# Weight loads ahead in groups of eight and four, and a new order for the first loads of a three-layer-plus-experts kernel

## The chip, the cores and the metric

The kernel runs on 1 core of one Trainium2 chip. The metric is the device time of one execution in microseconds (us), median of several runs. The engines are PE (TensorE, matmul), DVE (VectorE), ACT (ScalarE), POOL (GpSimd) and SP (SyncE, which here only issues DMAs); SPq and ACTq are the issuing sequencers of SP and ACT. Each engine works through its own list of instructions in order and waits on semaphores.

## The reference, cut to what matters

The input is 16 sequences of 256 tokens with 256 features. Four blocks follow each other, each behind a residual sum and a layernorm.

```
x = _layernorm(x + _L0_attn_ref(x, ...))   # projection by W_in, state-space scan in chunks, W_out
x = _layernorm(x + _L0_ffn_ref(x, ...))    # quantised gate/up/down, 704 hidden
x = _layernorm(x + _L1_attn_ref(x, ...))   # w_qkv, running sums over the tokens, swiglu with 1024 hidden
x = _layernorm(x + _L1_ffn_ref(x, ...))    # 16 experts, top 4 of each token, 448 hidden
def _L1_ffn_ref(x, W_up, W_gate, W_down, gate_inp):
    ...
    topv, topi = jax.lax.top_k(logits, K)
    w = jax.nn.softmax(topv.astype(jnp.float32), axis=-1).astype(x.dtype)
    ...
    u = jnp.einsum('nc,ehc->neh', xf, W_up)
    g = jnp.einsum('nc,ehc->neh', xf, W_gate)
    h = jax.nn.silu(g) * u
    y = jnp.einsum('neh,ech,ne->nc', h, W_down, dense_w)
```

## The kernel before, in words

The program has three blocks with a barrier of all engines between them.

`layers_block` computes the first three layers and the choice of experts, one sequence of 256 tokens (two tiles of 128) at a time. Each engine follows a list of its own, `ORDER`, written by hand; `run_skewed` goes through the list once a round. The first letter of an entry sets which sequence it works on: A the round's own, N, G+ or B3+ a later or earlier one, C two rounds back. So in round i the SP list does N0 (load of xT of sequence i+1), A0 (rows of x of sequence i), A2 (store of xg of sequence i), WL.0 to WL.5 (six pieces of the weights of expert i), C7 and C9 (stores of x3 and of its two bf16 parts, of sequence i-2) and CE.

Names that matter at the start. `loads` are eleven constants and weights (const is 1024 KB, w_in 1312 KB, w_out 512 KB) on the signal `setup_loaded`, for which PE, ACT and DVE wait before their first instruction. `loads_b` are ten weights of the later layers (w_sw alone 2048 KB, 6102 KB in all) on `weights_loaded`; they are first needed when sequence 0 reaches its second layer. `padding` and 17 stores of it fill the table `meta_dram`, with `padding_stored` waited for by the first scatter of POOL (D8). `xg` goes to DRAM and comes back as `xgs` by seven indirect gathers on POOL (AX), on the two signals `xgs_in`.

The weights of the experts are split into a high and a low bf16 part in the same rounds: SP loads a piece into `w_stage` (two buffers), ACT casts the high part (WH.k, line 998), DVE subtracts for the low part (WL.k, line 1476), SP stores it (`store_piece`) and right behind the store issues the load of the piece after next. ACT's list in the first round reads ... WH.0, A2S, F3, A2L, WH.1, A3, WH.2, WH.3, A3L, G1+ ...; A3L copies cb_cross and raises `cb_copied`, for which PE waits before A4.0 (the level matmuls of line 715) of the same sequence and before G1 of the next.

`experts_block` runs 144 tiles of 128 rows. For each, ACT loads its row of the table (`meta_in`), POOL gathers `xin`, SP turns it by a DMA transpose into `xh`, PE multiplies by the expert's weights in `w_all` (line 1656), SP turns the hidden part into `hh`, PE multiplies again (line 1671), POOL adds the rows into `sums_dram`. Tile i of the first sixteen waits for the weights of expert i. `load_weights` loads one expert by two DMAs of 896 and 448 KB. Before, experts 0 to 7 are loaded at the end of the round before the last, 8 to 13 behind the last stores of x (CE of sequence 15) and 14 and 15 at the start of `experts_block`. `combine_block` sums and normalises the rows at the end.

Of the kernel before, what the change touches and what calls it, by code (L numbers as in the profile page):

```python
# [24 lines left out]
P = 128  # L25
T = 256
NT = T // P
D = 256
DC = D // P
# [8 lines left out]
SH = 1024  # L38
# [12 lines left out]
EARLY_A, EARLY_B = 8, 14  # L51
# [120 lines left out]
def spread(ap, axis, n):  # L172
# [112 lines left out]
def layers_block(nc, ins, nseq, cap, ntile, ident, waited, small, base, table, meta_dram, x3_dram, sums_dram, split_ug, split_dn, xg_dram,  # L285
                 w_all, weights_in, w_start):
    with ExitStack() as ctx:
# [62 lines left out]
        w_sw = sb("w_sw", [P, DC, 2 * SH])  # L350
        w_so = sb("w_so", [P, SJ, D])
        x1 = sb("x1", [P, NT, D])
        x1T = sb("x1T", [P, DC, T])
        sg = sb("sg", [P, 2, T])
        hT = sb("hT", [P, SJ, T])
        x2 = sb("x2", [P, NT, D])
# [6 lines left out]
        den = sb("den", [P, NT, D])  # L363
        yc = sb("yc", [P, NT, D])
        assert nc.sbuf_base >= w_start + EARLY_B * WB
# [42 lines left out]
        def mat(k):  # L408
            return const[:, k, :]

        loads = [(const[:, :, :], ins["matrices"]), (ident, ins["matrices"][:, IDENT, :]), (small[:, :], ins["small"]),
                 (w_in[:, :, :], ins["w_in"].rearrange("(c p) n -> p c n", p=P)),
                 (dt_bias[:, :], ins["dt_bias"]), (neg_a[:, :], ins["a_log"]),
                 (bc_bias[:, :, :], ins["bc_bias"]), (chosen_rows[:, :], ins["chosen_rows"]), (halves[:, :, :, :], ins["halves"]), (right[:, :], ins["right"]),
# [10 lines left out]
                   (w_route[:, :, :], ins["w_route"].rearrange("(c p) n -> p c n", p=P))]  # L425
        setup_loaded = sig("setup_loaded", 16 * len(loads))
# [105 lines left out]
        def _(sp):  # L532
            sp_carrier = Carrier(sp, waited)
            for to, src in loads:
                sp.dma_start(to, src).then_inc(setup_loaded.sem, 16)

            def load_x(s):

                if later(s):
                    sp.wait_ge(z_projected.sem, z_projected.before(s))  # L540
                sp.dma_start(xT[:, :, :], ins["xT"].rearrange("(c p) t -> p c t", p=P)[:, :, bass.ds(s * T, T)]
                             ).then_inc(xT_in.sem, 16)

            def load_rows(s):
# [5 lines left out]
                if isinstance(s, int) and s == 0:  # L550
                    for to, src in loads_b:
                        sp.dma_start(to, src).then_inc(weights_loaded.sem, 16)
                    load_piece(0, 0)
                    load_piece(0, 1)

                    sp.dma_start(padding[:, :, :], ins["empty"]).then_inc(padding_in.sem, 16)
                    sp.wait_ge(nothing_set.sem, nothing_set.at(0))
                    for sums in sums_dram:
                        sp.dma_start(sums[nseq * T:nseq * T + P, :], nothing[:, 0:D]).then_inc(sums_cleared.sem, 16)
                    sp.wait_ge(padding_in.sem, padding_in.at(0))  # L560
                    for e in range(NE + 1):
                        sp.dma_start(meta_dram[e * cap:(e + 1) * cap, :].rearrange("(p i) w -> p i w", p=P),
                                     padding[:, :, :]).then_inc(padding_stored.sem, 16)
# [38 lines left out]
            def store_xg(s):  # L602
# [1361 lines left out]
```

## Time and profile before

| | |
|---|---|
| median of 3 runs | 2052.14 us (2052.07 to 2055.04) |
| the profiled execution | 2062.8 us, its span 2061.0 us |
| PE busy | 1773.3 us, 86% |
| DVE busy | 1320.1 us, 64% |
| POOL busy | 859.4 us, 42% |
| ACT busy | 730.7 us, 35% |
| DMA queue of SP | 171.79 MB, 32.5% of the 16 engines |
| DMA queue of POOL | 67.40 MB, 17.8% |

The span is the time from the first to the last instruction that the profile holds. Busy shares are averages over the three blocks, which have different limits: the first block ends near 1431 us of the span, the experts fill the rest up to the short last block.

### The profile page before, as it was taken

To read this page: it belongs to the slowest core of one execution; us is meant where nothing else is said; L and a number is where in the kernel's file an instruction comes from. 1 tells how busy PE (TensorE), PEld (TensorE's weight loads), DVE (VectorE), ACT (ScalarE), POOL (GpSimd) and SP (SyncE) were. 2 spreads that over 40 slices of the span, in tenths; PEclk is the share of its full clock that TensorE was granted. 3 is DMA by queue.
4 is the path that set the end of the run, shared out by engine and by line. 5 is a ranking of instruction groups with operands and counts; after the bars stand their busy time and mean duration, and the time that the engine had idled before them with its cause. 6 is when DMAs were issued, how large, how long until landed. Compare 5 with 4: busy or idle time off the path is not lost. (4 is left out here: it accounts for less than half of the span.)

```text
span 2061.0 us, 34901 instructions
## 1 busy us (share of the span) xinstructions
PE 1773.3 (86%) x8724; PEld 1226.6 (60%) x8725; DVE 1320.1 (64%) x2876; ACT 730.7 (35%) x1384; POOL 859.4 (42%) x856
## 2 busy tenths in 40 slices
PE   3589999989999899899998998872799999999980
PEld 2257667667576576676765766652456566666650
DVE  3778878778787788787877887621334444444445
ACT  3234344344343443443444434220222223233223
POOL 2123243333432432334324323222466676666654
PEclk8799999999999999999999999986899999999995
DMA  8123132231231321312313313277799999999997
GB/s 288 56 92 108 28 116 71 65 107 58 80 106 32 109 83 51 107 58 86 107 37 97 99 35 103 67 182 221 143 161 172 173 172 175 174 175 178 172 152 250
DMA packets 385800, 244.37 MB, mean 119 GB/s; under 512 B 269072, under 2 KB 364624, under 8 KB 385360
## 3 DMA queue, kind: packets, MB, share of 16 engines
q1 hardware_dynamic: 319952, 171.79, 32.5%
q0 software_dynamic: 40704, 67.40, 17.8%
q10 hardware_dynamic: 25088, 4.50, 1.2%
q8 instruction: 26, 0.43, 0.1%
q14 instruction: 30, 0.25, 0.0%
HBM read 119.23 MB, written 67.73 MB: 91 GB/s over the span
## 5 line engine op out<-in xcount | busy, mean ns | idle before, releaser
L1656 PE MATMUL pu<-w_all,xh 128*128 x1728 | 361.4, 356 | 59.4 <-DMA xh<-xin 44.0
L1656 PEld LDWEIGHTS pu<-w_all,xh 128*128 128x128 bf16 x1728 | 168.3, 98 | 209.9 <-issue 87.6
L1789 POOL DMA_INDIRECT sums_dram<-yo,meta_in x144 | 229.1, 1591 | 139.8 <-DVE yo L1756 68.3
L1742 DVE TENSOR_TENSOR hid<-pu,gate 128x448 f32<-128x448 f32 x144 | 90.0, 625 | 264.1 <-PE pu L1656 160.9
L819 PE MATMUL pb<-x1T,w_sw 128*128 128x256 f32 x1024 | 231.5, 383 | 0.8 <-ACT x1T L937 0.7
L819 PEld LDWEIGHTS pb<-x1T,w_sw 128*128 128x128 f32 x1024 | 193.8, 191 | 47.0 <-issue 16.2
L1671 PE MATMUL py<-w_all,hh 112*128 x1728 | 212.1, 272 | 1.4 <-DMA hh<-hs 1.4
L1671 PEld LDWEIGHTS py<-w_all,hh 112*128 112x128 bf16 x1728 | 168.5, 98 | 44.8 <-issue 1.9
L1776 POOL DMA_INDIRECT xin<-x_dram,meta_in x144 | 143.7, 998 | 66.5 <-issue 43.4
L635 PE MATMUL pa<-w_in,xT 128*128 128x512 f32 (+1 forms) x384 | 156.2, 552 | 14.5 <-DMA xT<-in_xT 13.8
L1306 DVE SCALAR_TENSOR_TENSOR y<-v,small,y 128x512 f32<-128x512 f32 x224 | 157.9, 746 | 1.2
L1719 ACT ACTIVATE hs<-hid 128x448 bf16<-128x448 f32 x144 | 83.0, 577 | 204.7 <-DVE hid L1742 158.0
L1124 POOL DMA_INDIRECT meta_dram<-meta,slot x128 | 131.9, 1031 | 49.3 <-issue 43.1
L1708 ACT ACTIVATE gate<-pu 128x448 f32<-128x448 f32 x144 | 78.4, 544 | 189.1 <-PE pu L1656 134.2
L1089 POOL DMA_INDIRECT xgs<-xg_dram,chosen_rows x112 | 115.5, 1031 | 59.8 <-issue 38.7
L715 PE MATMUL pa<-u,masked 128*128 128x512 f32 x224 | 113.2, 612 | 21.1 <-DVE masked L1256 16.2
L1025 POOL TENSOR_SCALAR yss<-yss 128x2 f32<-128x2 f32 x16 | 3.7, 230 | 306.1 <-ACT sq_a L924 306.1
L1756 DVE TENSOR_SCALAR yo<-py,meta_in 128x256 f32<-128x256 f32 x144 | 69.7, 484 | 87.3 <-PE py L1671 46.0
L977 ACT ACTIVATE sg<-pb 128x256 f32<-128x256 f32 x128 | 49.2, 384 | 203.9 <-PE pb L819 199.7
L635 PEld LDWEIGHTS pa<-w_in,xT 128*128 128x128 f32 x384 | 74.6, 198 | 77.4 <-issue 56.6
L1293 DVE TENSOR_TENSOR v<-pa,decay 128x512 f32<-128x512 f32 x128 | 85.0, 685 | 52.1 <-PE pa L715 49.6
L828 PE MATMUL pb<-w_so,hT 128*128 128x256 f32 x512 | 113.1, 379 | 0.0
(244 smaller groups left out, 3175.3 us busy)
## 6 DMA issues: line engine op xcount, KB each, us to landing
w_stage<-in_w_ug SPq DMA_DIRECT2D x64, 224.0 KB
split_ug<-w_parts SPq DMA_DIRECT2D x64, 224.0 KB
w_all<-split_ug SPq DMA_DIRECT2D x16, 896.0 KB, 10.5
xg_dram<-xg SPq DMA_DIRECT2D x16, 512.0 KB, 3.4
rows<-sums_dram SPq DMA_DIRECT2D x32, 256.0 KB, 5.4
w_stage<-in_w_dn SPq DMA_DIRECT2D x32, 224.0 KB
split_dn<-w_parts SPq DMA_DIRECT2D x32, 224.0 KB
w_all<-split_dn SPq DMA_DIRECT2D x16, 448.0 KB, 13.1
```

The lines of the kernel that those rows point to most:

```text
L635: last = mm(pa[:, bank + t, 0:width], xT[:, c, t * P:(t + 1) * P], w_in[:, c, first:first + width], start=c == 0, stop=c == DC - 1)
L715: mm(pa[:, n % 2, :], weights, u[:, n % US, :], start=True, stop=True).then_inc(level_done.sem, 1)
L819: last = mm(pb[:, 1 + j % 2, w * T:(w + 1) * T], w_sw[:, c, o:o + P], x1T[:, c, :], start=c == 0, stop=c == DC - 1)
L828: last = mm(pb[:, 3, t * D:(t + 1) * D], hT[:, j, t * P:(t + 1) * P], w_so[:, j, :], start=j == 0, stop=j == SJ - 1)
L1089: nc.gpsimd.indirect_dma_start(out=xgs[:, k, :], out_offset=None, in_=xg_dram, in_offset=bass.IndirectOffsetOnAxis(ap=chosen_rows[:, k:k + ...
L1124: nc.gpsimd.indirect_dma_start(out=meta_dram, out_offset=bass.IndirectOffsetOnAxis(ap=slot[:, t, j:j + 1], axis=0), in_=meta[:, t, j, :], ...
L1306: vec.scalar_tensor_tensor(y[:, t, :], v[:, n % 2, :], small[:, o:o + 1], y[:, t, :], ALU.mult, ALU.add).then_inc(y_added.sem, 1)
L1656: last = mm(pu[:, 2 * b + w, 0:EH], xh[:, m % XS, DC * xp + c, :], w_ug[:, bass.ds(e, 1), wp, c, w * EH:(w + 1) * EH], start=n == 0, stop= ...
L1671: last = mm(py[:, m % 2, 0:D], hh[0:EC, m % XS, EJ * hp + j, :], w_dn[:, bass.ds(e, 1), wp, j, :], start=n == 0, stop=n == 3 * EJ - 1)
L1742: vec.tensor_tensor(hid[:, :], pu[:, 2 * (m % 2), 0:EH], gate[:, :], ALU.mult).then_inc(hid_ready.sem, 1)
L1776: nc.gpsimd.indirect_dma_start(out=xin[:, b, :], out_offset=None, in_=x3_dram, in_offset=bass.IndirectOffsetOnAxis(ap=meta[:, m, 1:2], axis=0)
L1789: nc.gpsimd.indirect_dma_start(out=sums_dram[m % 2], out_offset=bass.IndirectOffsetOnAxis(ap=meta[:, m, 0:1], axis=0), in_=yo[:, m % XS, : ...
```

## The change

It has three parts. At the start, xT and w_in with the four small tensors that the first steps use are the first six DMAs, with a signal of their own for the first five behind xT; the rest of `loads` comes behind them, and the first users of const wait for it (PE and DVE in their first A2). The ten loads of `loads_b`, the padding, and its 17 stores move from the first `load_rows` into `load_rest`, behind the store of the first xg and behind a wait for the first seven gathers. At the end of the layers, experts 0 to 7 are loaded ahead of the stores of sequence 14, experts 8 to 11 behind them as soon as yc of the last sequence is there, none behind the last store, and experts 12 to 15 one by one between the first transposes of `experts_block`. Some buffers change place so that experts 8 to 11 lie over such as are free by then.

```diff
-EARLY_A, EARLY_B = 8, 14
+EARLY_A, EARLY_B = 8, 12
...
-    "SP": ("C7 A0 N0 A2 WL.0 WL.1 C9 WL.2 WL.3 WL.4 WL.5 CE"),
+    "SP": ("CE C7 A0 N0 A2 WL.0 WL.1 C9 WL.2 WL.3 WL.4 WL.5 CF"),
...
+        loads_first = [(w_in[:, :, :], ins["w_in"].rearrange("(c p) n -> p c n", p=P)), (small[:, :], ins["small"]),
+                       (dt_bias[:, :], ins["dt_bias"]), (neg_a[:, :], ins["a_log"]), (bc_bias[:, :, :], ins["bc_bias"])]
...
             def load_x(s):
 
                 if later(s):
                     sp.wait_ge(z_projected.sem, z_projected.before(s))
+                elif not at_start:
+                    return
...
-                    for to, src in loads_b:
-                        sp.dma_start(to, src).then_inc(weights_loaded.sem, 16)
                     load_piece(0, 0)
                     load_piece(0, 1)
...
+            def load_rest():
+
+                for part in xgs_in:
+                    sp.wait_ge(part.sem, part.at(0))
+                for to, src in loads_b:
+                    sp.dma_start(to, src).then_inc(weights_loaded.sem, 16)
+                sp.dma_start(padding[:, :, :], ins["empty"]).then_inc(padding_in.sem, 16)
+                sp.wait_ge(nothing_set.sem, nothing_set.at(0))
+                for sums in sums_dram:
+                    sp.dma_start(sums[nseq * T:nseq * T + P, :], nothing[:, 0:D]).then_inc(sums_cleared.sem, 16)
+                sp.wait_ge(padding_in.sem, padding_in.at(0))
+                for e in range(NE + 1):
+                    sp.dma_start(meta_dram[e * cap:(e + 1) * cap, :].rearrange("(p i) w -> p i w", p=P),
+                                 padding[:, :, :]).then_inc(padding_stored.sem, 16)
...
                 sp.dma_start(xg_dram.rearrange("(t p) d -> p t d", p=P), xg[:, :, :]).then_inc(xg_stored.sem, 16)
-
-            def load_early(s):
-
-                if isinstance(s, int) and s >= nseq - 2:
-                    if s == nseq - 2:
-                        for n in range(2):
-                            sp.wait_ge(piece_stored[n].sem, piece_stored[n].at(NE - 1))
-                        sp.wait_ge(x1_ready.sem, x1_ready.at(nseq - 1))
-                    for e in range(*((0, EARLY_A) if s == nseq - 2 else (EARLY_A, EARLY_B))):
+                if isinstance(s, int) and s == 0:
+                    load_rest()
...
+            def load_first(s):
+
+                if isinstance(s, int) and s == nseq - 2:
+                    for n in range(2):
+                        sp.wait_ge(piece_stored[n].sem, piece_stored[n].at(NE - 1))
+                    sp.wait_ge(x1_ready.sem, x1_ready.at(nseq - 1))
+                    for e in range(EARLY_A):
                         load_weights(sp, e, w_all, weights_in, split_ug, split_dn)
 
-            run_skewed(sp, ORDER["SP"], nseq, {"CE": load_early, "A2": store_xg, "N0": load_x, "A0": load_rows, "C7": store_x3, "C9": store_parts, "WL": store_piece})
+            def load_second(s):
+
+                if isinstance(s, int) and s == nseq - 2:
+                    sp.wait_ge(yc_ready.sem, yc_ready.at(nseq - 1))
+                    for e in range(EARLY_A, EARLY_B):
+                        load_weights(sp, e, w_all, weights_in, split_ug, split_dn)
...
-                    pe.wait_ge(setup_loaded.sem, setup_loaded.at(0))
+                    pe.wait_ge(first_loaded.sem, first_loaded.at(0))
...
-            for e in range(EARLY_B, NE):
-                load_weights(sp, e, w_all, weights_in, split_ug, split_dn)
 
             def step(r, m):
                 parts(r, m, 2, run=turn_x)
                 parts(r, m, 0, run=turn_h)
+                if isinstance(r, int) and UN * r + m + 2 < NE - EARLY_B:
+                    load_weights(sp, EARLY_B + UN * r + m + 2, w_all, weights_in, split_ug, split_dn)
```

The order of the instructions shows what the functions come to. First SP in the first round, between the last weight of the later layers and the first stored pieces of expert 0. Before (w_stage is filled by a piece's load, split_ug takes its store):

```order
L552 DMA w_route<-in_w_route 128x2x16
L585 DMA w_stage<-in_w_ug 128x448 x2
L556 DMA padding<-in_empty 128x132
L559 DMA sums_dram<-nothing 128x256 [waits nothing_set]
L559 DMA sums_dram<-nothing 128x256
L562 DMA meta_dram<-padding 128x132 [waits padding_in]
L562 DMA meta_dram<-padding 128x132 x16
L541 DMA xT<-in_xT 128x2x256 [waits z_projected]
L610 DMA xg_dram<-xg 128x2x512 [waits xg_ready]
L592 DMA split_ug<-w_parts 256x1x448 [waits piece_low]
L585 DMA w_stage<-in_w_ug 128x448
L592 DMA split_ug<-w_parts 256x1x448 [waits piece_low]
```

With the change, from the same two piece loads on:

```order
L590 DMA w_stage<-in_w_ug 128x448 x2
L542 DMA xT<-in_xT 128x2x256 [waits z_projected]
L615 DMA xg_dram<-xg 128x2x512 [waits xg_ready]
L560 DMA w_gate<-in_w_gate 128x2x704 [waits xgs_in1,xgs_in0]
L560 DMA w_up<-in_w_up 128x2x704
```

and, eight rows further on, behind the other weights:

```order
L560 DMA w_route<-in_w_route 128x2x16
L561 DMA padding<-in_empty 128x132
L564 DMA sums_dram<-nothing 128x256 [waits nothing_set]
L564 DMA sums_dram<-nothing 128x256
L567 DMA meta_dram<-padding 128x132 [waits padding_in]
L567 DMA meta_dram<-padding 128x132 x16
L597 DMA split_ug<-w_parts 256x1x448 [waits piece_low]
L590 DMA w_stage<-in_w_ug 128x448
```

The two piece loads stay early, the load of the second xT and the store of xg come ahead of the ten weights, and the first store of a piece, with the load of the third piece behind it, comes behind all of them.

Second, SP around the barrier between the layers and the experts. Before, the last of the loads that are issued in `layers_block`, the barrier, the last two experts and the first transposes:

```order
L1517 DMA w_all<-split_ug 128x3584 [waits weights_in1]
L1518 DMA w_all<-split_dn 112x2048
L287 UNCONDITIONAL_BRANCH [waits sums_cleared,x3_stored,piece_stored1,piece_stored0]
L1594 UNCONDITIONAL_BRANCH [waits barrier_Pool_Activation_PE_DVE_SP_release]
L1517 DMA w_all<-split_ug 128x3584 [waits weights_in2]
L1518 DMA w_all<-split_dn 112x2048
L1517 DMA w_all<-split_ug 128x3584 [waits weights_in3]
L1518 DMA w_all<-split_dn 112x2048
L1605 DMA_TRANSPOSE xh<-xin 128x4x128 [waits x_in0]
L1605 DMA_TRANSPOSE xh<-xin 128x4x128 [waits x_in1]
L1605 DMA_TRANSPOSE xh<-xin 128x4x128 [waits x_in2]
L1614 DMA_TRANSPOSE hh<-hs 128x8x128 [waits h_split]
```

With the change, from the last stores of x over the barrier on:

```order
L572 DMA sums_dram<-x 128x2x256 [waits x3_ready]
L574 DMA sums_dram<-nothing 128x2x256
L579 DMA x_dram<-x_parts 128x2x512 [waits x3_split]
L287 UNCONDITIONAL_BRANCH [waits sums_cleared,x3_stored,piece_stored1,piece_stored0]
L1619 UNCONDITIONAL_BRANCH [waits barrier_Pool_Activation_PE_DVE_SP_release]
L1630 DMA_TRANSPOSE xh<-xin 128x4x128 [waits x_in0]
L1542 DMA w_all<-split_ug 128x3584 [waits weights_in0]
L1543 DMA w_all<-split_dn 112x2048
L1630 DMA_TRANSPOSE xh<-xin 128x4x128 [waits x_in1]
L1542 DMA w_all<-split_ug 128x3584 [waits weights_in1]
L1543 DMA w_all<-split_dn 112x2048
L1630 DMA_TRANSPOSE xh<-xin 128x4x128 [waits x_in2]
```

The loads of experts 8 to 13 are gone from behind the last stores of x, and the first transposes stand ahead of the loads of experts 12, 13 and so on, one load behind each.

## Rows read from the trace of the kernel before

**Rows 1.** The page: span, and PE's busy tenths in 40 slices

```profile
span 2061.0 us, 34901 instructions
...
PE   3589999989999899899998998872799999999980
```

**Rows 2.** Timeline of SP, first round: start, duration, line, DMA

```profile
8.30 1.77 SPq L552 DMA_DIRECT2D w_gate<-in_w_gate  x1
...
16.05 8.10 SPq L552 DMA_DIRECT2D w_route<-in_w_route  x1
...
25.51 0.43 SPq L556 DMA_DIRECT2D padding<-in_empty  x1
...
31.64 7.92 SPq L562 DMA_DIRECT2D meta_dram<-padding  x17
...
40.16 0.38 SPq L610 DMA_DIRECT2D xg_dram<-xg  x1
40.92 0.65 SPq L592 DMA_DIRECT2D split_ug<-w_parts  x1
41.62 0.65 SPq L585 DMA_DIRECT2D w_stage<-in_w_ug  x1
```

**Rows 3.** Stretches at the start: busy by engine, PEclk, DMA share, GB/s

```profile
2.00:13.00 11.00, 0.00 (x0) 0.00 (x0) 0.00 (x0) 0.10 (x2) 0.00 (x0) 1.00 0.96 347
8.30:31.60 23.30, 13.04 (x31) 8.09 (x32) 9.79 (x36) 7.88 (x13) 1.21 (x2) 0.89 1.05 385
...
56.00:57.00 1.00, 0.00 (x0) 0.00 (x0) 0.86 (x2) 0.00 (x0) 0.00 (x0) 0.50 0.05 20
```

**Rows 4.** Timeline of PE, first round: start, us, instruction, wait before it

```profile
13.78 8.40 PE L635 MATMUL pa<-w_in,xT 128*128 128x288 f32 x16 [13.78 <-DMA xT<-in_xT]
...
29.54 5.43 PE L635 MATMUL pa<-w_in,xT 128*128 128x512 f32 x8
...
57.44 3.41 PE L715 MATMUL pa<-u,masked 128*128 128x512 f32 x4 [16.15 <-DVE masked L1256]
```

**Rows 5.** Timeline of POOL and ACT, first round

```profile
45.21 1.22 POOL L1089 DMA_INDIRECT xgs<-xg_dram,chosen_rows  x1 [7.24 <-issue]
45.91 0.58 ACT L998 ACTIVATE w_parts<-w_stage 128x448 bf16<-128x448 f32 x1 [5.61 <-DMA w_stage<-in_w_ug]
...
47.57 0.26 ACT L919 ACTIVATE cb_cross<-pa 128x128 f32<-128x128 f32 x1
```

**Rows 6.** Timelines of DVE and POOL, last sequence of the layers

```profile
1376.25 0.69 DVE L1394 TENSOR_TENSOR yc<-den,pb 128x512 f32<-128x512 f32 x1
...
1422.13 0.96 POOL L1124 DMA_INDIRECT meta_dram<-meta,slot  x1 [0.30 <-issue]
1431.78 0.31 POOL L1798 MEMSET hs<- 128x256 bf16 x1 [8.69 <-POOLq L287]
```

**Rows 7.** Timelines of ACT, POOL, SP and PE, first expert tiles

```profile
1432.76 12.52 ACTq L1701 DMA_DIRECT2D meta_in<-meta_dram  x6
...
1442.38 0.99 POOL L1776 DMA_INDIRECT xin<-x_dram,meta_in  x1 [10.29 <-DMA meta_in<-meta_dram]
...
1447.62 3.96 SPq L1605 DMA_TRANSPOSE xh<-xin  x3
...
1450.49 9.90 PE L1656 MATMUL pu<-w_all,xh 128*128 x36 [34.43 <-DMA xh<-xin]
...
1465.89 2.56 PE L1656 MATMUL pu<-w_all,xh 128*128 x12 [0.56 <-DMA xh<-xin]
```

**Rows 8.** DMA issues, 1330 to 1450 us: KB each, us to landing

```profile
x_dram<-x_parts SPq DMA_DIRECT2D x2, 256.0 KB, 2.3
```

**Rows 9.** Stretches at and after the end of the layers, columns as above

```profile
1377.00:1404.00 27.00, 23.10 (x100) 19.65 (x100) 5.09 (x13) 4.95 (x10) 0.94 (x2) 0.94 0.01 1
1408.00:1432.00 24.00, 1.57 (x10) 0.59 (x10) 6.63 (x37) 1.69 (x3) 8.06 (x9) 0.50 1.02 322
...
1600.00:1700.00 100.00, 95.79 (x635) 61.49 (x633) 43.19 (x80) 29.72 (x53) 68.91 (x54) 1.00 1.03 173
```

More of the change, by code:

```diff
@@ L363, in layers_block @@
         den = sb("den", [P, NT, D])
+        assert nc.sbuf_base >= w_start + EARLY_B * WB
+        w_sw = sb("w_sw", [P, DC, 2 * SH])
+        w_so = sb("w_so", [P, SJ, D])
+        x1T = sb("x1T", [P, DC, T])
+        sg = sb("sg", [P, 2, T])
+        hT = sb("hT", [P, SJ, T])
+        x2 = sb("x2", [P, NT, D])
         yc = sb("yc", [P, NT, D])
-        assert nc.sbuf_base >= w_start + EARLY_B * WB
         w_route = sb("w_route", [P, DC, NE])
@@ L409, in mat @@
             return const[:, k, :]
[L411 to L414, printed above, removed]
+        loads_first = [(w_in[:, :, :], ins["w_in"].rearrange("(c p) n -> p c n", p=P)), (small[:, :], ins["small"]),
+                       (dt_bias[:, :], ins["dt_bias"]), (neg_a[:, :], ins["a_log"]), (bc_bias[:, :, :], ins["bc_bias"])]
+        loads = [(const[:, :, :], ins["matrices"]), (ident, ins["matrices"][:, IDENT, :]),
+                 (chosen_rows[:, :], ins["chosen_rows"]), (right[:, :], ins["right"]), (halves[:, :, :, :], ins["halves"]),
                  (w_out[:, :, :], ins["w_out"].rearrange("(c p) n -> p c n", p=P))]
@@ L425, in layers_block @@
                    (w_route[:, :, :], ins["w_route"].rearrange("(c p) n -> p c n", p=P))]
+        first_loaded = sig("first_loaded", 16 * len(loads_first))
         setup_loaded = sig("setup_loaded", 16 * len(loads))
@@ L533, in _ @@
             sp_carrier = Carrier(sp, waited)
-            for to, src in loads:
-                sp.dma_start(to, src).then_inc(setup_loaded.sem, 16)
             def load_x(s):
@@ L550, in load_rows @@
                 if isinstance(s, int) and s == 0:
-                    for to, src in loads_b:
-                        sp.dma_start(to, src).then_inc(weights_loaded.sem, 16)
                     load_piece(0, 0)
                     load_piece(0, 1)
[L556 to L563, printed above, removed]
+            def load_rest():
[11 more added lines that the diff above has]
+                                 padding[:, :, :]).then_inc(padding_stored.sem, 16)
             def store_x3(s):
@@ L662, in a2 @@
             def a2(s):
+                if isinstance(s, int) and s == 0:
+                    pe.wait_ge(setup_loaded.sem, setup_loaded.at(0))
                 pe.wait_ge(steps_ready.sem, steps_ready.at(s))
@@ L1138, in _ @@
             cb_ = Chain(dve, dve_b.sem, DVE_B)
-            dve.wait_ge(setup_loaded.sem, setup_loaded.at(0))
+            dve.wait_ge(first_loaded.sem, first_loaded.at(0))
             dve.wait_ge(a_exp.sem, a_exp.at(0))
@@ L1144, in _ @@
             vec.tensor_scalar(bc_bias[:, 1, :], bc_bias[:, 1, :], float(N) ** -0.5, None, ALU.mult)
-            vec.tensor_copy(count_mats[:, :, :], const[:, STRICT:ONES + 1, :])
             vec.memset(base[:, :], 0.0)
@@ L1203, in a2 @@
             def a2(s):
+                if isinstance(s, int) and s == 0:
+                    dve.wait_ge(setup_loaded.sem, setup_loaded.at(0))
+                    vec.tensor_copy(count_mats[:, :, :], const[:, STRICT:ONES + 1, :])
                 ca.start(s)
```

16 lines of the change are left out of this document (9 added, 7 removed).

## The prediction, made before the changed kernel was run

> **What bounds the kernel now.** I read the page first: PE is busy in nine tenths of nearly every slice [rows 1]. Only three places are thin: the first slices, the step from the layers to the experts (about two thirds of the way) and the end. The change touches the first two, so it must be priced there, from the timelines. What the full middle adds is this: in it PE is fed by chains that each start from the round before, so a delay of the first round's chain should be carried to the end as it is, and a gain too.
>
> At the start PE's first matmul waits 13.78 us for xT, which lies behind all of `loads` [rows 4]. Then SP issues the ten later weights from 8.30 us, is held at w_route for 8.10 us, waits for the padding and issues 17 stores until 39.56 us; only then does xg go out, at 40.16 us, and the first piece of expert 0 at 40.92 us [rows 2]. POOL starts its gathers at 45.21 us, and PE stands idle for 16.15 us until 57.44 us [rows 4, 5]. At the step to the experts POOL's last scatter is issued by 1423.09 us, but the next block starts at 1431.78 us [rows 6]. The small table loads start at 1432.76 us and the first gather at 1442.38 us; the first transpose goes out at 1447.62 us and PE starts at 1450.49 us after 34.43 us of idling [rows 7]. All that while the DMA engines are full: share 1.02 at 322 GB/s [rows 9].
>
> **The change, part by part.**
>
> *First loads.* xT and `loads_first` are 1912 KB, 1.96 MB. The engines moved 347 GB/s from 2 us on [rows 3]; 2.0 + 1.96 / 0.347 = 7.6 us. The same sum for all that lay ahead before (4.09 MB) gives 13.8 us, which is the row. PE's start moves from 13.78 to about 7.9 us: -5.9 us. The rest of `loads` still lands near 13.8 us, and const is first used in A2 of PE, behind sixteen matmuls that took 8.40 us [rows 4], so not before 16.3 us: the new waits there cost nothing, and DVE's small cast that moved into A2 stands in its wait for PE.
>
> *xg.* SP now issues the second xT when z of sequence 0 is projected, at 29.54 + 5.43 - 5.9 = 29.1 us [rows 4], and the store of xg 0.56 us later, at 29.6 us instead of 40.16: the gathers start 10.5 us earlier, at 34.7 us. The last of the seven had landed by 56.1 us before (share 0.05 from 56 us) [rows 3], so `xgs_in` is complete at 45.6 us. Left there, PE's A4.0 would start 10.5 us earlier, too.
>
> *What stands behind it on SP.* SP is in order, and now everything else of the first round is queued behind that wait: ten weights (6102 KB), the padding (66 KB), its wait, 17 stores, and only then the first piece store and the load of the third piece. 6168 KB is 6.32 MB, at 385 GB/s [rows 3] 16.4 us, with 2.0 us for the start as above: the padding is in at 45.6 + 18.4 = 64.0 us. The 17 stores take 7.92 us [rows 2]: 72.0 us. From the end of the stores to the piece load's issue it was 41.62 - 39.56 = 2.1 us, of which the xT and the xg store took 1.1; now 1.0, so 73.0 us. The load took 45.91 - 41.62 = 4.3 us to where ACT casts it (WH.2) [rows 2, 5]: 77.3 us instead of 45.91. Before, this piece came in the shadow of PE's wait for the gathers; that cover is gone.
>
> *Who waits for it.* ACT is in order: behind WH.2 stand WH.3 and A3L, the copy of cb_cross, which ended at 47.83 us, 1.92 us after WH.2's start [rows 5]. PE's A4.0 waits for that copy, and DVE has its own WL.2 ahead of the second half of its level work. So A4.0 starts at 77.3 + 1.92 + 0.1 = 79.3 us instead of 57.44 us: **+21.9 us**. The 10.5 us won before it are spent. Everything later of the first rounds (the second projection, the vector work, the next xT, x_row and xg) hangs on this and moves along. Bounds: if the piece lands in the 2.3 us of a 256 KB store in a quiet stretch [rows 8], 2 us less; if the rate is 10% better or worse, 1.6 us either way; and PE may start cold again, as it did at 57 us (PEclk 0.50 just before) [rows 3], up to 2 us more. The term is 18 to 26 us.
>
> The Trainium skill (DMA: Bandwidth & Descriptors, section Bandwidth) gives a core about 358 GB/s from HBM. The row shows 385 GB/s over 23.3 us, above it; by the page the term would be 1.3 us more. The measurement decides.
>
> *Experts 0 to 7 ahead of the stores of sequence 14.* They start when x1 of sequence 15 is there, as before. The two stores wait behind them for some 27 us; they are next asked for at the last sequence's x3, near 1404 us. Nothing.
>
> *Experts 8 to 11.* They wait for yc, done at 1376.94 us [rows 6], and 5.5 MB at 322 GB/s take 17 us. From 1377 to 1404 us the DMA share was 0.01 [rows 9]. Nothing, and hidden by 27 us of matmuls.
>
> *None behind the last store.* The last scatter, issued by 1423.09 us, now lands in a quiet machine. With 2.0 us for it (2.3 us for a 256 KB store [rows 8]) and 0.2 for the barrier the block starts at 1425.3 instead of 1431.78: -6.5 us. The table load took 1442.38 - 1432.76 = 9.6 us; at 2.3 us: -7.3. Gather to transpose took 5.24 us; with 0.99 us of issue and 2.1 us to land: -2.1. So PE's first expert matmul comes up to 15.9 us earlier relative to the layers.
>
> *Experts 12 to 15 between the transposes.* These are still 5.5 MB, 17.1 us at 322 GB/s, and they now stand ahead of the transposes of tiles 1 to 4. If they cost only themselves, tile 4 of PE follows the first transpose's end (1447.62 - 15.9 + 3.96 / 3 = 1433.0 us on the old clock) by 17.1 us and the 2.9 us from transpose to PE [rows 7], at 1453.0 us against 1465.89: -12.9 us. If the tiles' own transfers add up with them (a tile takes a full 3.6 us of DMA at share 1.03 later on [rows 9]; up to tile 4 about two thirds of four tiles, 9.6 us, its own transpose among it), tile 4 comes at 1459.7 us: -6.2 us. From there on the engines are full either way, and the experts' stage also has a DMA share of 1.03, so part of a lead may be given back. I take **-9 us**, between the two and nearer to the second, with -13 to -3 as bounds.
>
> The Trainium skill (DMA: Bandwidth & Descriptors, Queues, rings and completion order) says that descriptors of one row are consumed in ring order and that an engine takes turns between rows packet by packet. By the first half the transposes, on SP's row with the loads, wait for all of them, the second of my two cases. By the second half a 2 KB table load on ACT's row should hardly be held up; the row shows 9.6 us, so it is.
>
> **The sum.** 2061.0 + 21.9 - 9 = 2073.9 us of span. The profiled execution took 2062.8 us, the median of the others 2052.14; I take the same difference off: 2052.1 + 12.9 = **2065 us**, 0.6% slower. A difference of under 0.2%, 4 us, can't be told from none.
>
> **Rivals.**
> *The stall does not reach the end (faster).* One mechanism: the third piece is ready before ACT and PE need it, or the lost time is taken up by idle stretches of the first two rounds. Then the 10.5 us at the gathers stay won and the step to the experts adds 9: 2052.1 - 19.5 = 2033 us. It decides the sign when the third piece's cast starts before about 64 us: A4.0 comes 2.0 us later, at 66.4, which is 9 us behind its old place, what the experts' step pays for. For it: PE has idle time in the first slices [rows 1]. Against: between the gathers and that cast stand 6.3 MB, a landed wait and 17 issues on one queue, and that idle time consists of waits along the same chain. Chance 0.12.
> *The stall is shorter and the experts' step gives all it can (no change).* 18 or less at the start, -13 at the end: 2052 to 2057 us. For it: the DMA engines start empty this time. Chance 0.12.
> *The experts' step gives nothing.* The four loads ahead of the first transposes, and a stage that is bound by DMA afterwards, give the lead back, as ring order would have it: +22 - 1, 2073 us. For it: DMA share 1.03; against: the idle DMA time after 1446 us is filled now. Chance 0.16.
> *My forecast*, 2057 to 2072 us: 0.60.
>
> **Numbers.** The range reaches from the no-change case to the case without a gain at the experts, 2054 to 2075 us; what is left out is the faster rival and a little at both sides, 0.2. Faster by over 4 us: 0.12 and 0.02 from the shorter stall, 0.14. Within: 0.10. Slower: 0.76.
>
> **What the profile would show.** PE's first matmul near 8 us; xg stored near 30 us and the seven gathers from 35 us; w_gate issued near 46 us and the 17 stores near 64 to 72 us; ACT's WH.2 near 77 us with a wait for the load of w_stage of some 35 us or more, PE's A4.0 near 79 us. Every later landmark of the layers 20 to 24 us later than before (the last scatter issued near 1445 us). No DMA before the barrier, which comes 2 us after that scatter; a table load of 2 to 3 us; the first expert tiles spaced by 4 to 6 us. I am wrong if A4.0 comes before 64 us, if the landmarks at 1404 us moved by less than A4.0 did, or if the loads of experts 12 to 15 hold the tiles beyond the fifth.

## The result, and the profile after

The changed kernel took 2079.38 us, median of 4 runs (2074.37 to 2085.55), beside 2053.59 us for the kernel before in 4 runs (2052.07 to 2063.79). The ratio is 1.0124, with an interval of 1.0095 to 1.0154: 25.8 us slower, 19.5 to 31.6. The same two kernels measured again on another occasion (in the experiments, e9) gave 1.0101 (1.0065 to 1.0136), 19.1 us slower. The direction and the place were forecast. The forecast difference of 12.9 us was too small, and 2079.38 us is outside the range of 2054 to 2075; the second measurement, put on the 2052.1 us of the forecast, would have been inside it.

The profiled execution of the changed kernel took 2074.37 us, and its page begins so (the span, and the busy tenths of PE in 40 slices):

```profile
span 2072.6 us, 34903 instructions
...
PE   3379999899999999999999999874799999999980
```

Against [rows 1] the second and third slice, 52 to 155 us, have fallen from 5 and 8 to 3 and 7. The step to the experts, near slice 28, is a little fuller. The spans differ by 11.6 us only, far less than the medians; why a single pair of profiles misleads here stands in the last section.

The first round in the timelines of the changed kernel, for SP, POOL, ACT and PE in turn (start, duration, instruction, and in brackets the wait before it and what ended it); they answer to [rows 2, 4, 5]:

```profile
0.73 0.46 SPq L542 DMA_DIRECT2D xT<-in_xT  x1
...
30.65 0.39 SPq L615 DMA_DIRECT2D xg_dram<-xg  x1
48.43 0.37 SPq L560 DMA_DIRECT2D w_gate<-in_w_gate  x1
...
53.41 5.96 SPq L560 DMA_DIRECT2D w_route<-in_w_route  x1
59.42 1.87 SPq L561 DMA_DIRECT2D padding<-in_empty  x1
...
67.45 7.92 SPq L567 DMA_DIRECT2D meta_dram<-padding  x17
75.50 0.65 SPq L597 DMA_DIRECT2D split_ug<-w_parts  x1
76.19 0.61 SPq L590 DMA_DIRECT2D w_stage<-in_w_ug  x1
...
35.11 1.25 POOL L1112 DMA_INDIRECT xgs<-xg_dram,chosen_rows  x1 [2.80 <-issue]
...
43.67 0.95 POOL L1112 DMA_INDIRECT xgs<-xg_dram,chosen_rows  x1 [0.30 <-issue]
...
79.18 0.58 ACT L1021 ACTIVATE w_parts<-w_stage 128x448 bf16<-128x448 f32 x1 [43.73 <-DMA w_stage<-in_w_ug]
...
81.48 0.26 ACT L942 ACTIVATE cb_cross<-pa 128x128 f32<-128x128 f32 x1
...
8.32 7.41 PE L656 MATMUL pa<-w_in,xT 128*128 128x288 f32 x16 [8.32 <-DMA bc_bias<-in_bc_bias]
...
81.99 3.75 PE L738 MATMUL pa<-u,masked 128*128 128x512 f32 x4 [45.12 <-ACT cb_cross L942]
```

PE starts 5.5 us earlier and xg goes out 9.5 us earlier than before. Then SP has nothing to show between 30.65 + 0.39 and 48.43 us: it stands in the wait for the gathers. Behind it run the weights, the padding and 17 stores. The first piece of expert 0 is stored at 75.50 instead of 40.92 us although ACT and DVE had made it long before. The last two brackets are the chain. ACT waited 43.73 us for the third piece and PE 45.12 us for ACT's copy of cb_cross, which stands behind the cast. The stretches say what the DMA engines did meanwhile (stretch, length, busy time and count of PE, PEld, DVE, ACT, POOL, then PEclk, DMA share, GB/s):

```profile
46.00:47.00 1.00, 0.00 (x0) 0.00 (x0) 0.85 (x2) 0.00 (x0) 0.00 (x0) 0.50 0.48 184
47.00:48.00 1.00, 0.00 (x0) 0.00 (x0) 0.97 (x1) 0.00 (x0) 0.00 (x0) 0.50 0.05 12
49.00:66.00 17.00, 0.00 (x0) 0.00 (x0) 0.00 (x0) 0.00 (x0) 0.00 (x0) 0.50 1.00 363
```

The last gather landed by 47 us. Then come 17 us of weights at full share, with PE, DVE, ACT and POOL not busy at all.

The step to the experts in the same kernel, POOL and ACT's queue, SP, and PE; it answers to [rows 6, 7]:

```profile
1441.84 0.95 POOL L1147 DMA_INDIRECT meta_dram<-meta,slot  x1 [0.30 <-issue]
1446.69 0.31 POOL L1823 MEMSET hs<- 128x256 bf16 x1 [3.89 <-POOLq L287]
1450.21 1.00 POOL L1801 DMA_INDIRECT xin<-x_dram,meta_in  x1 [3.21 <-DMA meta_in<-meta_dram]
...
1447.67 6.12 ACTq L1726 DMA_DIRECT2D meta_in<-meta_dram  x6
...
1453.14 1.33 SPq L1630 DMA_TRANSPOSE xh<-xin  x1
1454.54 0.57 SPq L1542 DMA_DIRECT2D w_all<-split_ug  x1
1455.15 0.42 SPq L1543 DMA_DIRECT2D w_all<-split_dn  x1
1455.70 1.46 SPq L1630 DMA_TRANSPOSE xh<-xin  x1
...
1456.62 4.66 PE L1681 MATMUL pu<-w_all,xh 128*128 x12 [20.84 <-DMA xh<-xin]
1462.37 4.22 PE L1681 MATMUL pu<-w_all,xh 128*128 x12 [1.08 <-DMA xh<-xin]
1466.82 2.44 PE L1681 MATMUL pu<-w_all,xh 128*128 x12 [0.23 <-DMA xh<-xin]
1472.47 4.13 PE L1681 MATMUL pu<-w_all,xh 128*128 x12 [3.20 <-DMA xh<-xin]
1476.43 1.48 PE L1696 MATMUL py<-w_all,hh 112*128 x12
1479.88 1.31 PE L1681 MATMUL pu<-w_all,xh 128*128 x6 [1.98 <-DMA xh<-xin]
```

From the last scatter's issue to the first expert matmul it is 1456.62 - 1441.84 = 14.8 us, where it was 28.4 us [rows 6, 7]. The loads of expert 12 stand between the first two transposes; tile 0 needed 3.5 us from transpose to PE, tile 1 needed 1462.37 - 1455.70 = 6.7 us. The fifth tile (tile 4) starts on PE 1479.88 - 1441.84 = 38.0 us behind the scatter, against 1465.89 - 1422.13 = 43.8 us before [rows 6, 7]: of the 13.6 us of lead 5.7 are left. The stretches of these tiles:

```profile
1458.00:1463.00 5.00, 3.92 (x11) 1.42 (x10) 0.86 (x2) 1.12 (x2) 0.20 (x1) 0.50 1.09 339
...
1468.00:1473.00 5.00, 1.80 (x10) 0.91 (x10) 1.89 (x3) 1.12 (x2) 0.94 (x1) 0.98 1.12 358
```

So the DMA engines, which the change had left idle ahead of the first tile, are full again within the first four.

### The profile page after: what moved, and what is told of

Read it like the earlier page. It is cut to its first block and busy times, and to the rows that moved or that the text cites. A ratio compares the mean times of both kernels' runs of the same rounds, so it can differ in the third digit from the quotient of the medians.

```text
span 2072.6 us, 34903 instructions
## 1 busy us (share of the span) xinstructions
PE 1773.5 (86%) x8724; PEld 1228.1 (59%) x8725; DVE 1327.8 (64%) x2876; ACT 730.2 (35%) x1384; POOL 861.4 (42%) x856
## 3 DMA queue, kind: packets, MB, share of 16 engines
q0 software_dynamic: 40704, 67.40, 17.4%
## 5 line engine op out<-in xcount | busy, mean ns | idle before, releaser
L1112 POOL DMA_INDIRECT xgs<-xg_dram,chosen_rows x112 | 119.1, 1063 | 57.4 <-issue 34.4
L1781 DVE TENSOR_SCALAR yo<-py,meta_in 128x256 f32<-128x256 f32 x144 | 69.7, 484 | 86.7 <-PE py L1696 45.6
```

The costliest lines, as they stand in the source:

```text
L1112: nc.gpsimd.indirect_dma_start(out=xgs[:, k, :], out_offset=None, in_=xg_dram, in_offset=bass.IndirectOffsetOnAxis(ap=chosen_rows[:, k:k + ...
```

## The experiments

Two questions were open. The first is which half the loss comes from: theory S says from the start, with a gain at the experts; its rival E says that the loads between the first transposes cost time as well. The second is what in the start costs: the order on SP, where a wait holds all that is queued behind it, or the transfers themselves, which would take their 17 us anywhere. (The recorded expectations call the two sides of each question theory A and theory B or rival.) Each run was timed beside the kernel before on the same chip.

| run | median us (range, runs) | before us | ratio (interval) | us |
|---|---|---|---|---|
| e1 new start alone | 2075.36 (2061.74-2078.46, 6) | 2052.43 | 1.0110 (1.0061-1.0158) | +22.9 |
| e2 new end alone | 2049.46 (2036.99-2058.82, 12) | 2052.43 | 0.9997 (0.9969-1.0025) | -3.0 |
| e3 e1, table filled early | 2064.72 (2050.48-2068.36, 14) | 2052.43 | 1.0063 (1.0037-1.0088) | +12.3 |
| e4 whole change, table early, weights spread | 2043.33 (2032.43-2053.84, 12) | 2052.43 | 0.9967 (0.9937-0.9996) | -9.1 |
| e5 e1, table early, spread behind the gathers | 2050.4 (2044.1-2061.82, 12) | 2058.49 | 0.9964 (0.9946-0.9982) | -8.1 |
| e6 e2, four loads later | 2053.33 (2046.74-2059.81, 12) | 2058.49 | 0.9970 (0.9950-0.9990) | -5.2 |
| e7 e5 with the end of e6 | 2048.89 (2040.58-2056.54, 12) | 2058.49 | 0.9949 (0.9930-0.9969) | -9.6 |
| e8 e1, one call moved | 2063.39 (2053.38-2069.64, 12) | 2058.49 | 1.0022 (0.9998-1.0046) | +4.9 |
| e9 the change again | 2063.63 (2058.99-2072.18, 6) | 2044.56 | 1.0101 (1.0065-1.0136) | +19.1 |
| e10 e1 again | 2066.08 (2062.53-2073.2, 6) | 2044.56 | 1.0114 (1.0078-1.0149) | +21.5 |
| e11 e5 with the change's own end | 2036.81 (2029.8-2042.56, 12) | 2044.56 | 0.9957 (0.9937-0.9978) | -7.8 |

The last column is the difference of the medians; the ratio is a comparison of its own over the same runs, and for e2 the two differ (0.9997 is -0.6 us).

**e1, the new start alone.** The end is put back as it was: experts 8 to 13 behind the last stores of x, 14 and 15 ahead of the first transpose.

```diff
-EARLY_A, EARLY_B = 8, 12
+EARLY_A, EARLY_B = 8, 14
...
-            def load_first(s):
...
-            def load_second(s):
+            def load_early(s):
...
+            for e in range(EARLY_B, NE):
+                load_weights(sp, e, w_all, weights_in, split_ug, split_dn)
...
             def step(r, m):
...
-                if isinstance(r, int) and UN * r + m + 2 < NE - EARLY_B:
-                    load_weights(sp, EARLY_B + UN * r + m + 2, w_all, weights_in, split_ug, split_dn)
```

> The new first loads and the later weights behind the gathers, with the old end of the layers and the old loads of the experts. Theory A (the third piece of expert 0 holds ACT and PE in the first round, and this delay is carried to the end; the end part is a gain): slower than before by 24 to 28 us, PE's A4.0 near 82 us, layers' last scatter some 26 us later than before. Theory B (most of the measured 26 us come from the loads of experts 12 to 15 among the first transposes or from the moved buffers): slower by 12 us or less.

It took 22.9 us more than before, 21.5 in its second measurement (e10). A4.0 started at 81.34 us and POOL began to make the third sequence's xg at 207.85 us, as in the changed kernel (81.99 and 210.87 us). That is a little under the 24 to 28 us of theory A and above the 12 us of theory B, though the lower end of the interval is 12.5 us.

**e2, the new end alone**, the same edits the other way round, on the kernel before.

```diff
-EARLY_A, EARLY_B = 8, 14
+EARLY_A, EARLY_B = 8, 12
...
-    "SP": ("C7 A0 N0 A2 WL.0 WL.1 C9 WL.2 WL.3 WL.4 WL.5 CE"),
+    "SP": ("CE C7 A0 N0 A2 WL.0 WL.1 C9 WL.2 WL.3 WL.4 WL.5 CF"),
...
-            for e in range(EARLY_B, NE):
-                load_weights(sp, e, w_all, weights_in, split_ug, split_dn)
...
+                if isinstance(r, int) and UN * r + m + 2 < NE - EARLY_B:
+                    load_weights(sp, EARLY_B + UN * r + m + 2, w_all, weights_in, split_ug, split_dn)
```

> The old start, with experts 0 to 7 ahead of the stores, 8 to 11 behind yc, and 12 to 15 among the transposes. Theory A: faster than before by 3 to 9 us, block start 6 us after nothing but the last scatter, tiles 1 to 4 spaced by 4 to 6 us. Theory B: slower by 10 us or more. Together with the first run: under theory A the two differences add up to that of the whole change within 3 us.

The medians differ by -3.0 us, and the interval (-6.4 to +5.1 us) does not tell it from nothing. The first expert matmul came 14.7 us behind the last scatter, so the early part of the gain is there; most of it does not reach the end. E falls as an account of the loss: by its interval the end costs 5 us at most. S holds for the place of the loss. The sum of e1 and e2, +19.9 us, is 5.9 us short of the first measurement of the change and not within the 3 us that I had set; it is within 1 us of the second (e9).

**e3, the table filled early.** The padding load and the 17 stores go into the stretch in which SP is idle anyway, behind the first two pieces. The wait for the gathers and the ten weights stay.

```diff
                     load_piece(0, 0)
                     load_piece(0, 1)
+                    fill_table()
...
-            def load_rest():
+            def fill_table():
 
-                for part in xgs_in:
-                    sp.wait_ge(part.sem, part.at(0))
-                for to, src in loads_b:
-                    sp.dma_start(to, src).then_inc(weights_loaded.sem, 16)
                 sp.dma_start(padding[:, :, :], ins["empty"]).then_inc(padding_in.sem, 16)
...
+            def load_rest():
+
+                for part in xgs_in:
+                    sp.wait_ge(part.sem, part.at(0))
+                for to, src in loads_b:
+                    sp.dma_start(to, src).then_inc(weights_loaded.sem, 16)
```

> As the start alone, but the padding, its wait and its 17 stores go out in SP's idle stretch between 8.5 and 30 us; the ten weights stay behind the gathers and ahead of the first piece store. Theory A in its detailed form (SP's order and one ring for SP's loads): the piece load is issued near 60 us, as w_route's issue ends at 59.4, but lands behind the ten weights, near 67 to 68 us; ACT's third cast is 11 to 12 us earlier than in the start alone, and the time is better than the start alone by 11 to 12 us, still slower than before by 13 to 17. Rival (the piece passes the weights on the engines): cast near 64 us, better by 15. Rival (the 17 stores' own traffic is what hurts): no change against the start alone.

The timelines of SP, ACT and PE in e3:

```profile
59.60 0.61 SPq L593 DMA_DIRECT2D w_stage<-in_w_ug  x1
...
66.12 0.58 ACT L1018 ACTIVATE w_parts<-w_stage 128x448 bf16<-128x448 f32 x1 [31.53 <-DMA w_stage<-in_w_ug]
...
68.26 3.52 PE L735 MATMUL pa<-u,masked 128*128 128x512 f32 x4 [32.69 <-ACT cb_cross L939]
```

The piece's load is issued at 59.60 instead of 76.19 us and is cast 6.5 us later, when the weights ahead of it have landed, where the changed kernel took 3.0 us in a quiet machine. A4.0 comes 13.7 us earlier than in the changed kernel, and the time falls from +22.9 to +12.3 us, just under the 13 to 17 forecast. So some 11 to 14 us of the term were the landed wait and the 17 issues, and the rest the weights ahead of the piece.

**e4, the whole change with the weights spread.** The table as in e3, no wait for the gathers, and the ten weights in groups behind the piece stores of expert 0 (`WL.k`), the first two from the second piece on.

```diff
+LATER = (0, 0, 2, 6, 7, 8, 10)
...
                 elif not isinstance(e, int) or e + 1 < NE:
                     load_piece(e + 1, k + 2 - WP)
+                if isinstance(e, int) and e == 0:
+                    for to, src in loads_b[LATER[k]:LATER[k + 1]]:
+                        sp.dma_start(to, src).then_inc(weights_loaded.sem, 16)
...
-                if isinstance(s, int) and s == 0:
-                    load_rest()
```

> The whole change, but the table's padding and stores in SP's idle stretch near the start and the ten later weights spread behind the stores of the pieces of expert 0. Theory A: nothing stands ahead of the third piece, the 10 us won at the gathers stay won and the end's 5 us are added: 12 to 17 us faster than before, near 2038 us, A4.0 near 47 us. Rival (the first round's idle time takes up what is won as well as what is lost): no more than 5 us faster.

It is 9.1 us faster than before: the same sets of loads, and the sign has turned. The forecast was more, 12 to 17 us, and A4.0 near 47 us; it came at 52.06. DVE and PE of e4:

```profile
47.71 1.90 DVE L1308 TENSOR_TENSOR u<-xgs,from_first 128x512 f32<-128x512 f32 x3 [8.85 <-DMA xgs<-xg_dram,chosen_rows]
...
52.06 3.75 PE L737 MATMUL pa<-u,masked 128*128 128x512 f32 x4 [14.90 <-DVE masked L1280]
```

A4.0 now hangs on the gathers, as before the change, and DVE waits 8.85 us for them: w_gate and w_up, issued from 39.33 us on, run beside them. That these two hold the gathers up is what e5 goes on to test.

**e5, the start alone, spread behind the gathers.** As e4 without the new end, and the first weights one place later.

```diff
-LATER = (0, 0, 2, 6, 7, 8, 10)
+LATER = (0, 0, 0, 2, 7, 8, 10)
```

> Start only, old end: table in SP's idle stretch, the later weights spread behind the stores of the third to sixth piece of expert 0, none while the gathers run. In the fourth run w_gate and w_up ran beside the gathers and A4.0 came at 52.1 us. Theory (the gathers' landing sets A4.0 once the third piece is out of the way): A4.0 at 47 to 49 us, 9 to 10 us earlier than before, and the time 7 to 11 us under before's. Rival (a lead in the first round is taken back by the round that follows): 3 us or less.

DVE and PE of e5:

```profile
43.96 1.90 DVE L1301 TENSOR_TENSOR u<-xgs,from_first 128x512 f32<-128x512 f32 x3 [5.99 <-DMA xgs<-xg_dram,chosen_rows]
...
48.31 3.68 PE L730 MATMUL pa<-u,masked 128*128 128x512 f32 x4 [12.24 <-DVE masked L1273]
```

The gathers are in 3.75 us earlier than in e4 (0.8 us of it because they were issued earlier, from 34.98 and not 35.76 us) and A4.0 starts at 48.31 us, 9.1 us ahead of the kernel before. The time is 8.1 us below it, within the forecast. This is the gain of the first loads that the change earned and then spent.

**e6 and e7, the four loads later.** On e2, experts 12 to 15 go out behind the transposes of steps 3, 5, 7 and 9 instead of -2 to 1. e7 is this end with the start of e5.

```diff
-                if isinstance(r, int) and UN * r + m + 2 < NE - EARLY_B:
-                    load_weights(sp, EARLY_B + UN * r + m + 2, w_all, weights_in, split_ug, split_dn)
+                if isinstance(r, int) and UN * r + m in (3, 5, 7, 9):
+                    load_weights(sp, EARLY_B + (UN * r + m - 3) // 2, w_all, weights_in, split_ug, split_dn)
```

> The old start and the new end, but experts 12 to 15 are loaded behind the transposes of tiles 3, 5, 7 and 9 and not behind the first four. Theory A (the four loads, in ring order ahead of the transposes of tiles 1 to 4, take back the 10 to 14 us by which the first tile is early): last scatter to the fourth down product 38 to 42 us and not 48 to 49, and the time 6 to 10 us under the second run's. Theory B (the experts' stage is bound by its DMAs, whatever their order): the early tiles are faster, but the last down product still comes 574 us behind the last scatter, and the time is that of the second run within 3 us.

> The fifth and the sixth run together. Under theory A of the sixth 15 to 20 us faster than before, under theory B 9 to 13.

PE of e6:

```profile
1433.56 9.93 PE L1663 MATMUL pu<-w_all,xh 128*128 x36 [20.77 <-DMA xh<-xin]
...
1460.05 4.11 PE L1663 MATMUL pu<-w_all,xh 128*128 x12 [3.40 <-DMA xh<-xin]
...
1481.18 3.78 PE L1663 MATMUL pu<-w_all,xh 128*128 x12 [4.19 <-DMA xh<-xin]
```

The first three tiles now run in one piece, 36 matmuls in 9.93 us. But the waits that stood between them are back later, 3.40 and 4.19 us, each followed by a slower twelve matmuls (4.11 and 3.78 us, where twelve take 2.44 elsewhere). The last down product came 578.7 us behind the last scatter, 578.8 in e7, against 574 to 581 us with the loads at the first tiles. e6 measured 5.2 us below the kernel before, its interval reaches from 2 to 10 us, so that it overlaps e2's; and e7's -9.6 us (9 to 13 under theory B) stands beside e5's -8.1 of the same occasion. So the times are those of theory B: where the four loads go among the first dozen tiles makes no difference that these runs can tell.

**e8, the order of SP alone.** On e1 the whole of `load_rest`, with its wait, weights, padding and stores, is called behind WL.1 of expert 0 instead of behind the store of xg. All transfers are the same.

```diff
+                if isinstance(e, int) and e == 0 and k == 1:
+                    load_rest()
...
-                if isinstance(s, int) and s == 0:
-                    load_rest()
```

> Start only, old end, with one call moved: the ten weights, the padding and the 17 stores wait for the gathers as in the change, but stand behind the loads of the third and fourth piece. Same transfers, same waits. If it is SP's order alone that costs: A4.0 at 48 to 50 us; the fifth piece is now the one that is late (cast near 78 us, with ACT's copy of xs behind it, at 74.3 us before), so the time is 3 to 7 us over before's instead of 23. If the traffic or the wait for the gathers costs: 15 us or more over before's.

PE and ACT of e8:

```profile
49.35 3.75 PE L731 MATMUL pa<-u,masked 128*128 128x512 f32 x4 [11.94 <-DVE masked L1274]
...
80.81 0.63 ACT L1014 ACTIVATE w_parts<-w_stage 112x512 bf16<-112x512 f32 x1 [23.53 <-DMA w_stage<-in_w_dn]
```

A4.0 is at 49.35 us, and the stall has moved to the fifth piece, where ACT waits 23.53 us. Of the +22.9 us of e1, +4.9 are left (-0.4 to +9.5). The transfers were not the cost; what stood behind SP's wait, was. This is the test that parts the two, and both numbers, A4.0 and the time, came as forecast for SP's order.

**e9, e10 and e11, on a third occasion**: the change and e1 once more, unchanged, and the start of e5 with the end of the change.

> The changed kernel itself once more, with more runs. If the terms are +24 at the first round and -3 to -6 at the experts: 18 to 22 us over before's median. If the first measurement of it (25.8 us, four runs) holds: 24 or more, and something in it adds to what the two parts do alone.

> The start alone once more (first 22.9 us over before). 22 to 26 us over before's median, and 3 to 6 us over the whole change.

> The spread start of the fifth run with the change's own end (12 to 15 behind the first four transposes). If the parts add: 11 to 15 us faster than before, 3 to 6 us faster than the fifth run, and no slower than the seventh, whose late loads ended 579 us behind the last scatter against 574 here.

The change lost 19.1 us and its start alone 21.5 (22 to 26 forecast), so the end brought 2.4 us (3 to 6 forecast), after 3.0 us in e2. e11 has the lowest median of all, 2036.81 us, 7.8 us below the kernel before (4.5 to 12.9) and less than the 11 to 15 I had forecast. It beats both kernels. Whether it beats e4, e5 or e7 can't be said from these runs, since they were timed on other occasions. Beside e5 (-8.1) the new end adds nothing that shows.

## Why the prediction was wrong in size

**The start, +21.9 forecast.** Right in each step, and each a little later than forecast (us):

| | forecast | measured |
|---|---|---|
| PE's first matmul | 7.9 | 8.32 |
| xg stored | 29.6 | 30.65 |
| first gather | 34.7 | 35.11 |
| w_gate issued | 45.6 | 48.43 |
| the 17 stores ended | 72.0 | 75.4 |
| third piece issued | 73.0 | 76.19 |
| third piece cast | 77.3 | 79.18 |
| A4.0 | 79.3 | 81.99 |

At w_gate, the gathers had started 0.4 us later, landed within 11.9 instead of 10.9 us, and 1.4 us went by from there to the issue. Four kernels with this start have A4.0 at 81.4 us on average, the three with the old start at 58.0: +23.4. The delay is carried: POOL makes the third sequence's xg at 208.2 us on average with it (206.0 to 210.9) and 185.2 without (183.5 to 187.1), **+22.9 us**. Timed alone it costs 22.9 and 21.5 us. The ten weights moved at 363 GB/s, less than the 385 of [rows 3]. Weights and padding are 6.32 MB, 17.4 us at that rate instead of 16.4; from w_gate's issue to the first table store it was 67.45 - 48.43 = 19.0 us where I gave 18.4. The section that I weighed, of the Trainium skill (DMA: Bandwidth & Descriptors, section Bandwidth), gives a core about 358 GB/s from HBM, and says of that figure that it is for both cores of a pair streaming. The 363 GB/s here are near it, the 385 of [rows 3] above it.

One of my own signs of being wrong did appear: the last scatter came 19.7 us later in the profiled pair, less than the 24.6 us of A4.0. The thirteen rounds between had nothing changed in them and were 8.7 us shorter in this one profile (last section). Over all the kernels the delay of A4.0, +23.4 us, and that of the third xg, +22.9 us, agree.

**The end, -9 forecast.** This is the term that failed, in size: "Experts 12 to 15 between the transposes", taken at -9 us. I priced three savings ahead of PE's first expert matmul, 15.9 us together. They measured 28.4 - 14.8 = 13.6 us in the profiled pair: the barrier 4.8 instead of 6.5 (POOL waited 3.89 us on the quiet machine, where I gave 2.2; the table load 7.1 of the forecast 7.3, gather to transpose 2.3 of 2.1), less 0.6 us by which the first transpose itself took longer. Over all kernels it was 14.7 or 14.8 us with the new end and 24.5 to 28.7 with the old. What comes out at the far end is less. From the last scatter to the last down product the five kernels with the change's own end took 575.9 us on average (573.7 to 580.9), the six with the old one 580.3 (574.1 to 586.3): **-4.4 us**, with a spread that lets it be anything from nothing to the forecast 9; the profiled pair alone would give 8.7. The timed differences say 3.0 (e2) and 2.4 us (e9 against e10).

Where the lead goes can be followed tile by tile. DVE reads each tile's up product when PE has made it (hid<-pu). The lead is the old end's average time from the last scatter to that instruction, less the new end's (at the fifth tile the single kernels lie between 41.4 and 47.3 us with the old end, 39.7 and 42.3 with the new):

| lead in us at tile (counted from 1) | 1 | 3 | 4 | 5 | 8 | 12 | 20 | 64 | 144 |
|---|---|---|---|---|---|---|---|---|---|
| the change's end, five kernels | 12.2 | 8.9 | 5.4 | 3.8 | 3.9 | 3.2 | 3.1 | 3.6 | 4.4 |
| the loads later, e6 and e7 | 12.3 | 12.2 | 12.3 | 12.4 | 5.4 | 0.5 | 0.8 | 1.7 | 1.6 |

With the four loads between the first transposes the lead is spent by the fifth tile. With the loads later it lasts until they come, and is spent then. From there on it neither shrinks nor grows by more than about a microsecond, so the four loads take it, wherever they stand among the first tiles. The long stage behind them gives nothing back: between 1480 and 2040 us PE waited 24.5 us before and 25.4 us with the change. The DMA share of 1.03 in that stage, for which I had written that "part of a lead may be given back", was therefore the wrong place to look. The choice between my two cases was the step that failed. The second, in which the tiles' own transfers add up with the loads, gave -6.2 us at the fifth tile, and the profiled pair shows -5.7; averaged over the kernels it is -3.8. My "between the two" leaned on the first case, in which the loads cost only themselves, and no run with the loads in that place shows it.

**The sum.** 22.9 - 4.4 = +18.5 us, and e9 measured +19.1. The first measurement says +25.8, with 19.5 as the lower end of its interval, and it had four runs on either side; the two intervals overlap (+19.5 to +31.6 and +13.3 to +27.8), and no part of the kernel was found in which the 7 us between them are lost. So of the 12.9 us by which the first measurement exceeds the forecast, 4.6 are the term at the experts, 1.0 the start, and the rest stays open. That it fell outside the stated range, and e9 would not have, can't be told from chance. My third rival ("the experts' step gives nothing", +21) was nearer than my forecast. It deserved more of the chance, though of its two reasons only the four loads hold: the tiles show no lead given back in the stage behind them.

**The rival on the other side.** A stall that does not reach the end did not come about: it would have needed the cast before 64 us, and it came at 79.18. e3, with the cast at 66.12 us, bears out its price for the start: A4.0 was 10.8 us behind the kernel before, and the time +12.3. But 64 us leaned on the 9 us of the experts' step; with 4.4 the sign would turn when A4.0 is 4.4 us late, at a cast near 57.4 + 4.4 - 2.0 = 59.8 us (worked out, not tried). e5 and e8, with A4.0 9.1 and 8.1 us ahead of the kernel before, show that most of the 10.5 us forecast at the gathers was real, and was lost only to what SP had queued behind a wait.

## What to carry to other kernels

A wait in the list of an engine that issues DMAs in order is paid by everything that stands behind it, so ask of each later entry who needs it first; here one small piece load, put behind such a wait, ten weights and 17 stores, cost 23 us, and moving the same call two entries down gave back some 18. Bulk loads go behind the entries that feed a chain, a few at a time and clear of the gathers (e4 against e5: some 3 us at the vector work). A head start won by moving loads behind the first tiles is not worth its length at the first instruction: the moved loads still have to pass (12.2 us at the first tile, 3.8 at the fifth, 4.4 at the end). Price it at the first tile behind the last of them.

## What was unexpected in the hardware

**Rounds of the same work differ in length.** The thirteen rounds behind the third xg took 79.3 to 82.2 us each in the changed kernel. Two of them, as stretches from POOL's making of xg to the next (columns as before):

```profile
210.87:290.14 79.27, 75.08 (x331) 54.44 (x330) 66.96 (x146) 33.91 (x68) 30.40 (x33) 1.00 0.26 82
...
372.05:454.25 82.20, 76.37 (x330) 54.80 (x329) 65.14 (x146) 33.85 (x67) 28.69 (x34) 0.98 0.26 78
```

The timeline of PE at the w_qkv group of each:

```profile
241.93 3.70 PE L807 MATMUL pb<-w_qkv,x1T 128*128 128x512 f32 x8 [0.69 <-ACT x1T L960]
...
404.19 5.40 PE L807 MATMUL pb<-w_qkv,x1T 128*128 128x512 f32 x8 [0.69 <-ACT x1T L960]
```

The two groups as stretches:

```profile
241.90:245.60 3.70, 3.67 (x9) 1.76 (x10) 3.63 (x8) 3.05 (x7) 1.20 (x2) 1.00 0.00 0
404.20:408.00 3.80, 3.80 (x5) 1.64 (x6) 3.73 (x8) 2.40 (x4) 1.20 (x2) 0.55 0.00 0
```

The same eight matmuls behind the same 0.69 us of waiting took 3.70 us at a granted clock of 1.00, the 2.4 GHz level, and 5.40 us at 0.55, near the 1.2 GHz level. That is 1.7 of the 2.9 us by which the rounds differ, 79.27 and 82.20 us; where the rest goes was not followed. Ahead of both groups PE had idled alike (1.24 and 1.43 us, a short transpose, then 0.69), and at a granted clock of 1.00, so what decides it is left open. Over the kernels, the thirteen rounds up to the last xg took 1045 to 1063 us with nothing changed in them, and the profile of before was one of the long ones (1063.3, the changed kernel 1054.6). That is why the profiled pair misleads: the third xg is 27.4 us late in it, the rounds take back 8.7 and the experts another 8.7, and small differences elsewhere make it 11.6 us, of a loss of 19 to 26.

**An issue behind many large loads is held.** The issue of the tenth weight, w_route, took SP 5.96 us in the changed kernel, 8.10 before [rows 2] and 7.06 in e3. It is the smallest but one of the ten (16 KB), and the nine before it took 0.4 to 0.7 each in the changed kernel. With the weights spread, in e5, the same issue took 0.61 us:

```profile
85.02 0.61 SPq L605 DMA_DIRECT2D w_route<-in_w_route  x1
```

So it is the place behind the others and not the transfer; that a queue is full then is the likely reading, and no run shows its depth.

**A small load is slow beside another engine's large ones.** The 2 KB table load, issued by ACT, took 9.6 us from its issue to POOL's gather with SP's loads running [rows 7] and 1450.21 - 1447.67 = 2.5 us without.
